# Attention on one core: products for the row maxima issued in pairs behind pairs of score products

## The chip, the cores and the metric

The kernel runs on one core of one Trainium2 chip. The metric is the device time of one execution in microseconds (us). The median of three runs of the kernel before is 5910.59 us (5900.03 to 5910.8).

## The reference

4096 tokens of width 256 go through two layers. What matters here is the attention, which is computed three times: once in the first layer, in a sparse form, and twice in the second layer, in a full causal form.

```
L0:  scores of a query against its own block of 128 keys and every 8th key of all tokens; causal; softmax
L1a: rotary attention:   softmax(causal(Q K^T / 4)) V
L1b: RMS-normed Q and K: softmax(causal(Q K^T / 4)) V
```

Each has 16 heads of width 16. Around them stand layer norms, a quantised product, projections and four experts with a top-2 router; the change doesn't touch them.

## The kernel before, in words

The program runs in stages one after the other: an embedding stage, `attend` for the sparse attention (job 0), a middle stage, `attend` for the two dense attentions together (jobs 1 and 2), and the experts. Only `attend` (L480) is touched, and it is used for both the sparse and the dense stage.

**Units and steps.** A unit is 4 heads (a group) by 512 queries (a strip, number j). The sparse stage has 32 units, the dense stage 64 (8 groups of 8 strips; j runs up in one group and down in the next). A unit is cut into steps of 128 keys: 4(j+1) steps in the dense stage, 1152 in all, and 5 in the sparse one, 160 in all. The last four steps of a dense unit are diagonal: their products are narrower and have a small triangle product added.

**What a step does.** TensorE makes four score products, one for each head, called S0 to S3 below (L712 dense, L719 sparse), with keys as rows and queries as columns. S0 and S1 fill one pair of PSUM banks, S2 and S3 the other (banks 0 to 3). ScalarE takes the exponential of one pair at a time (L770). TensorE then multiplies the exponentials with the values in fp32 (the "weigh" product, called W below, L750, bank 4), one step behind the scores.

**The maxima.** The scores are products of bf16 parts with 96 rows; the softmax needs the maximum of every query row before the exponentials. So every score is made a second time with queries as rows and keys as columns: a "tile" of 128 queries by up to 512 keys, called T below (L686 dense, L676 sparse, L689 and L677 for the masks), and VectorE reduces it to one maximum per row (L799 dense, L789 to L795 sparse). This runs ahead of the scores by `lead(n)` steps, mostly 36 in the dense stage. The tiles go through three PSUM banks in turn (banks 5 to 7): entry e uses bank 5 + e % 3 and waits (L668) until VectorE has finished with entry e - 3. Two other kinds of entry share these three banks, once in each unit: "hand" (L694), which turns the finished negated maxima so that they can be written into the three extra rows of the queries, and "out" (L698), which turns the finished output for the division.

**The order of the work** is written out once as a list, `order` (L506 to L545), which TensorE, VectorE and SyncE all walk. `emit_tiles(goal)` (L510) appends tiles until `goal` of them stand in the list. Inside a step the call at L537 comes behind every score product, with a goal that is one higher each time. So a usual step of TensorE reads S0 T0 S1 T1 S2 T2 S3 T3 W. The first step of a unit has no W behind its products, and the last has two. "out" is appended behind S3 of the second step of a unit (L535), "hand" behind the sixth tile of a unit (L519), and "negate" (L523), VectorE's five small operations that form the negated maximum, behind a unit's last tile.

Of the kernel before, what the change touches and what calls it, by code (L numbers as in the profile page):

```python
# [76 lines left out]
def _build(nc, ctx, d, out):  # L77
# [402 lines left out]
    def attend(jobs, stage, splits, past):  # L480
# [17 lines left out]
        def lead(n):  # L498
            if sparse:
                return sizes[0] + 2  # L500
            if n >= len(units) - STRIPS:
                return sizes[n] + 4
            return min(max(sizes) + 4, 10 + int((2 * BLOCKS * (ends[n] - sizes[n])) ** 0.5))
# [6 lines left out]
        def emit_tiles(goal):  # L510
            nonlocal at
            while at < min(goal, len(ahead)):
                n, tile = ahead[at]
                first_tile = at == 0 or ahead[at - 1][0] != n
                if first_tile:
                    order.append(("queries", n + 1, None))
                order.append(("tile", n, tile))
                of_unit = at - 4 * (ends[n] - sizes[n])
                if of_unit == 5 and n >= 1:  # L519
                    order.append(("hand", n - 1, None))  # L520
                at += 1
                if at == 4 * ends[n]:
                    order.append(("negate", n, None))  # L523
                    if n == len(units) - 1:
                        order.append(("hand", n, None))

        for n in range(len(units)):
            emit_tiles(4 * (ends[n] - sizes[n] + lead(n)))
            emit_tiles(4 * ends[n] + 6)
            order.append(("unit", n, None))  # L530
            for c in range(sizes[n]):
                m = ends[n] - sizes[n] + c
                for h in range(GROUP):
                    order.append(("score", n, (m, c, h)))
                    if n >= 1 and c == 1 and h == 3:  # L535
                        order.append(("out", n - 1, None))
                    emit_tiles(4 * (m + lead(n)) + h + 1)  # L537
                if c >= 1:
                    order.append(("weigh", n, (m - 1, c - 1)))
            order.append(("weigh", n, (m, c)))  # L540
            if n == 0 or n % STRIPS == STRIPS - 1:
                group = 1 if n == 0 else n // STRIPS + 2
                if group < len(groups):
                    order.append(("keys", group, None))
# [8 lines left out]
        with ExitStack() as st:  # L553
# [283 lines left out]
            def attend_pool():  # L837
                tiles, loaded, chunks = splits
                for i, (src, high, low) in enumerate(chunks):
# [15 lines left out]
    middle_early = ExitStack()  # L855
    stage3 = [sbuf(middle_early, f"stage3_{i}", [P, 3 * DIM]) for i in range(2)]
    attend((0,), "sparse", (stage3, [sem(f"stage3_in{i}") for i in range(2)], [
        chunk for name, src, n_out in (("wproj0", d["L0_attn_c_proj_w"], DIM), ("w_rotary", d["L1_attn_Wqkv"], 3 * DIM),
                                       ("w_moe_qkv", d["moe_qkv"], 3 * DIM))
# [495 lines left out]
    for tile, src in ((wo[:], d["L1_ffn_wo"].rearrange("(c p) n -> p c n", p=P)[:, :, MASKED:DIM]),  # L1355
                      (wp[:], d["L1_attn_Wproj"].rearrange("(c p) n -> p c n", p=P)),
                      (n2[:], d["L1_ffn_n2_w"].partition_broadcast(P)), (lower[:], d["c_lower"])):
        sp.dma_start(tile, src).then_inc(final_weights, 16)
    attend((1, 2), "dense", (stage5, [sem(f"stage5_in{i}") for i in range(2)], [
        chunk for name, n_out in (("gate_w", EXPERTS), ("e0_up", HID), ("e2_l1", HID), ("e1_w1", HID), ("e1_w2", HID))  # L1360
        for chunk in matrix(early, name, d["L1_ffn_" + name], DIM, n_out)]), GROUPS * STRIPS)
# [485 lines left out]
```

How the kernel before makes its waits and increments, by code:

```python
    def settle(self):  # L56
        self.engine.wait_ge(self.sem, self.n)
# [56 lines left out]
    def stage_end(finals):  # L114
        for engine in (pe, dve, act, pool, sp):
            for last_sem, value in finals:
                engine.wait_ge(last_sem, value)
# [60 lines left out]
        def embed_sp():  # L178
# [9 lines left out]
                              (scales[:, 0:1], d["L0_ffn_input_scale"].partition_broadcast(P)),  # L188
                              (scales[:, 1:2], d["L0_ffn_kernel_scale"].partition_broadcast(P))):
                sp.dma_start(tile, src).then_inc(weights_in, 16)
            w_view = d["L0_attn_c_attn_w"].rearrange("(c p) n -> p c n", p=P)
            for c in range(DC):
                sp.dma_start(stage[c][:], w_view[:, c, :]).then_inc(stage_in[c], 16)
            for s in range(STRIPS):
                if s + 1 < STRIPS:
                    n = s + 1
                    if n >= 3:
                        sp.wait_ge(base_stored[n % 3], 16 * (n // 3))
                    sp.dma_start(xs[n % 3][:], rows_of(d["L0_attn_hidden_states"], n)).then_inc(x_in[n % 3], 16)
                sp.wait_ge(v_biased, 4 * (s + 1))
                for g in range(GROUPS):
                    dst = v_d[0][g, s * STRIP:(s + 1) * STRIP, :].rearrange("(b p) n -> p b n", p=P)
                    sp.dma_start(dst, ves[s % 2][:, :, g * GROUP * GCOL:(g + 1) * GROUP * GCOL]).then_inc(v_stored[s % 2], 16)
                sp.wait_ge(p3_set, 2 * (s + 1))
                for i, part in enumerate((p1, p2, p3)):
```

## Time and profile before

| | |
|---|---|
| median of three runs | 5910.59 us |
| profiled execution | 5916.0 us |
| its span, first to last instruction | 5914.2 us |
| mean granted TensorE clock | 0.909 of full speed |
| TensorE busy | 5481.3 us, 93% |
| VectorE busy | 4209.3 us, 71% |
| ScalarE busy | 2931.1 us, 50% |

The span's stages, by the groups of instructions and the slices: embedding to about 300 us, sparse attention to about 1370 us, the middle stage to about 1810 us, dense attention to about 5170 us, experts to the end. In the rows below PE is TensorE's matmul, PEld its weight load, DVE VectorE, ACT ScalarE, SP SyncE. A matmul's row lasts from its issue to its modelled end, so rows of neighbouring matmuls overlap; the chain of work gives each only the time by which it moves the end on.

### The profile page before, as it was taken

How to read it: one execution, taken by the hardware profiler on the slowest of the kernel's cores; microseconds unless marked ns; L12 is line 12 of the kernel's file. 1: busy time of each engine (PE TensorE's matmuls, PEld its weight loads, DVE VectorE, ACT ScalarE, POOL GpSimd, SP SyncE). 2: the span in 40 equal slices, each digit the busy share in tenths (PEclk: the TensorE clock that was granted, in tenths of full speed). 3: DMA queues.
4: the chain of work that ended last, by engine and by line, in shares of the span. 5: the costliest groups of instructions: out<-in, count | busy, mean ns of one | idle time of the engine just before them, and what ended most of it. 6: DMA issues, size and time to landing. Idle time of an engine off the chain costs nothing.

```text
span 5914.2 us, 80510 instructions
## 1 busy us (share of the span) xinstructions
PE 5481.3 (93%) x32000; PEld 2459.4 (42%) x32000; DVE 4209.3 (71%) x8394; ACT 2931.1 (50%) x3357; POOL 327.1 (6%) x304
## 2 busy tenths in 40 slices
PE   5499999997665999999999999999999999899999
PEld 4333333334552333333333333333333333378888
DVE  7554444455775888888888888888888887465555
ACT  3223233333332556666666666666666666622332
POOL 2100000001550000000000000000000000020000
PEclk8667677788876999999999999999999999989999
DMA  3631312002546002002002002020120000110110
GB/s 119 143 59 23 50 22 45 19 15 79 161 146 117 15 10 45 12 19 50 9 8 44 11 19 49 8 43 9 19 51 8 8 8 8 30 56 19 36 36 8
DMA packets 268674, 242.18 MB, mean 41 GB/s; under 512 B 73213, under 2 KB 247805, under 8 KB 264061
## 3 DMA queue, kind: packets, MB, share of 16 engines
q1 hardware_dynamic: 268296, 237.02, 17.9%
q8 instruction: 253, 4.15, 0.3%
q14 instruction: 125, 1.02, 0.1%
HBM read 143.49 MB, written 92.27 MB: 40 GB/s over the span
## 4 chain that ended last, share of the span: by engine, by line
PE 84%; DVE 8%; SPq 2%; ACT 2%; issue 2%; DMA 1%; POOL 0%; ACTq 0%; DVEq 0%; POOLq 0%
PE psum L750 21%; PE psum L712 17%; PE psum L686 16%; PE psum L73 12%; PE psum L676 7%; PE psum L719 3%; DVE maxes_dense L799 2%; PE psum L698 1%; SPq L604 1%; PE psum L715 1%; PE psum L689 1%; PE psum L1485 1%; SPq L590 1%; PE psum L724 1%; PE psum L722 1%
## 5 line engine op out<-in xcount | busy, mean ns | idle before, releaser
L799 DVE TENSOR_REDUCE maxes_dense<-psum 128x1 f32<-128x512 f32 (+3 forms) x4608 | 2708.3, 640 | 509.0 <-PE psum L686 296.6
L770 ACT ACTIVATE probs_dense<-psum 128x1024 f32<-128x1024 f32 (+3 forms) x2304 | 2100.5, 951 | 1108.1 <-PE psum L712 820.4
L686 PE MATMUL psum<-keys_dense,queries_dense 96*128 96x512 bf16 (+3 forms) x4608 | 1692.7, 369 | 68.3 <-DMA queries_dense<-parts_scratch 55.8
L712 PE MATMUL psum<-queries_dense,keys_dense 99*128 99x512 bf16 (+3 forms) x4608 | 1668.6, 367 | 8.1 <-ACT probs_dense L770 6.8
L750 PE MATMUL psum<-probs_dense,values_dense 128*32 128x512 f32 (+3 forms) x9216 | 1133.9, 569 | 0.0
L712 PEld LDWEIGHTS psum<-queries_dense,keys_dense 99*128 99x128 bf16 x4608 | 448.0, 98 | 1164.9 <-ACT probs_dense L770 878.4
L686 PEld LDWEIGHTS psum<-keys_dense,queries_dense 96*128 96x128 bf16 x4608 | 452.0, 98 | 532.2 <-DVE maxes_dense L799 260.4
L676 PE MATMUL psum<-keys_sparse,queries_sparse 96*128 96x512 bf16 x512 | 545.4, 1070 | 53.4 <-DMA queries_sparse<-parts_scratch 53.4
L789 DVE TENSOR_REDUCE maxes_sparse<-psum 128x1 f32<-128x144 f32 (+23 forms) x512 | 221.8, 433 | 485.1 <-PE psum L677 485.0
L770 ACT ACTIVATE probs_sparse<-psum 128x1024 f32<-128x1024 f32 x224 | 229.2, 1025 | 483.4 <-PE psum L727 174.0
L1592 ACT ACTIVATE activated<-psum 128x512 f32<-128x512 f32 x208 | 124.5, 599 | 421.5 <-PE psum L73 410.3
L750 PEld LDWEIGHTS psum<-probs_dense,values_dense 128*32 128x32 f32 x9216 | 187.5, 108 | 349.6 <-issue 300.2
L719 PE MATMUL psum<-queries_sparse,keys_sparse 99*128 99x512 bf16 x512 | 241.1, 474 | 23.6 <-DMA queries_sparse<-neg_rows_sparse 22.9
L689 PE MATMUL psum<-tri_query,ident_bf 128*128 128x128 bf16 x1024 | 227.1, 222 | 0.0
L715 PE MATMUL psum<-tri_key,ident_bf 128*128 128x128 bf16 x1024 | 224.6, 221 | 0.0
L719 PEld LDWEIGHTS psum<-queries_sparse,keys_sparse 99*128 99x128 bf16 x512 | 73.9, 146 | 351.2 <-issue 296.9
L791 DVE TENSOR_REDUCE maxes_sparse<-psum 128x1 f32<-128x496 f32 (+9 forms) x496 | 205.6, 415 | 0.0
L1727 DVE CAST hid_high<-activated 128x512 fp32r<-128x512 f32 x208 | 91.5, 440 | 144.8 <-ACT activated L1592 142.0
L750 PE MATMUL psum<-probs_sparse,str_values 128*32 128x512 f32 x1024 | 192.2, 834 | 0.0
L770 ACT ACTIVATE probs_sparse<-psum,after_bias 128x1024 f32<-128x1024 f32 x96 | 106.5, 1115 | 157.3 <-PE psum L719 157.3
L1771 POOL CAST e_down_high<-stage 128x192 fp32r<-128x192 f32 (+1 forms) x10 | 3.6, 358 | 2764.4 <-DMA stage<-in_L_ffn_e_down 2764.4
L1729 DVE TENSOR_TENSOR hid_low<-activated,hid_high 128x512 fp32r<-128x512 f32 x208 | 150.5, 723 | 7.2
(297 smaller groups left out, 5834.9 us busy)
## 6 DMA issues: line engine op xcount, KB each, us to landing
parts_scratch<-part SPq DMA_DIRECT2D x72, 512.0 KB, 4.1
v_scratch<-ve_s SPq DMA_DIRECT2D x96, 256.0 KB, 2.8
queries_dense<-parts_scratch SPq DMA_DIRECT2D x384, 64.0 KB
keys_dense<-parts_scratch SPq DMA_DIRECT2D x42, 512.0 KB, 17.2
keys_sparse<-parts_scratch SPq DMA_DIRECT2D x24, 512.0 KB, 18.9
queries_sparse<-parts_scratch SPq DMA_DIRECT2D x192, 64.0 KB
ao_scratch<-aos_dense SPq DMA_DIRECT2D x64, 128.0 KB, 2.0
ao_s<-ao_scratch SPq DMA_DIRECT2D x16, 512.0 KB, 4.7
```

Of the source, the lines that this page charges most:

```text
L73: m = pe.matmul(out_ap, left(l, c), right(r, c), start=(n == 0), stop=(n == len(pairs) - 1))
L676: pe.matmul(bank, q[0:TROWS, h, b * P:(b + 1) * P], k[0:TROWS, h, STRIDE - 1::STRIDE], start=True, stop=False)
L686: m = pe.matmul(bank[:, 0:width], q[0:TROWS, h, b * P:(b + 1) * P], k[0:TROWS, h, kc * STRIP:kc * STRIP + width], start=True, stop=kc != j)
L689: m = pe.matmul(bank[:, b * P:(b + 1) * P], ident_bf[:], tri_query[:], start=False, stop=True)
L712: m = pe.matmul(full[:, first_col:STRIP], k[:, h, c * P:(c + 1) * P], q[:, h, first_col:STRIP], start=True, stop=not diagonal)
L715: m = pe.matmul(full[:, first_col:first_col + P], ident_bf[:], tri_key[:], start=False, stop=True)
L719: m = pe.matmul(full, k[:, h, c * P * STRIDE + STRIDE - 1:(c + 1) * P * STRIDE:STRIDE], q[:, h, :], start=True, stop=not partly)
L750: m = pe.matmul(psum[own_rows, 4, cols], vt, probs[(2 * m_at + h // 2) % 6][:, h % 2, cols], start=(c == 0), stop=(c == sizes[n] - 1 and b ...
L770: act.activation(probs[i % 6][:, :, first_col:STRIP], psum[:, at2:at2 + 2, first_col:STRIP], ACT.Exp, scale=SCALE, **extra).then_inc(exp_d ...
L789: m = dve.tensor_reduce(mx[:, h * BLOCKS + b, 0:1], bank[:, 0:after], AX.X, ALU.max)
L791: m = dve.tensor_reduce(mx[:, h * BLOCKS + b, 2:3], bank[:, after:NSTR], AX.X, ALU.max)
L799: m = dve.tensor_reduce(mx[:, h * BLOCKS + b, kc:kc + 1], bank[:, 0:width], AX.X, ALU.max)
```

## The change

Inside a step the tiles are appended behind the second and the fourth score product only. The goal there is the same as before, so each call appends two tiles.

```
                     order.append(("score", n, (m, c, h)))
                     if n >= 1 and c == 1 and h == 3:
                         order.append(("out", n - 1, None))
-                    emit_tiles(4 * (m + lead(n)) + h + 1)
+                    if h % 2 == 1:
+                        emit_tiles(4 * (m + lead(n)) + h + 1)
                 if c >= 1:
                     order.append(("weigh", n, (m - 1, c - 1)))
```

A usual step of TensorE reads S0 S1 T0 T1 S2 S3 T2 T3 W. Every instruction is kept, with its operands; the entries keep their order among each other but for "out", which now comes ahead of both tiles T2 and T3 of its step, where it came between them.

## Rows read from the trace of the kernel before

**Rows 1.** The page: busy times, and the granted clock in 40 slices of 148 us.
```profile
PE 5481.3 (93%) x32000; PEld 2459.4 (42%) x32000; DVE 4209.3 (71%) x8394; ACT 2931.1 (50%) x3357; POOL 327.1 (6%) x304
PEclk8667677788876999999999999999999999989999
```

**Rows 2.** Busy time by stretch: stretch, us, busy by engine (instructions), clock, DMA share, GB/s.
```profile
444.00:592.00 148.00, 148.00 (x721) 48.60 (x720) 71.09 (x187) 47.41 (x48) 5.28 (x4) 0.76 0.11 24
...
1036.00:1184.00 148.00, 148.00 (x683) 49.43 (x680) 69.93 (x182) 45.79 (x46) 0.00 (x0) 0.70 0.09 18
...
2072.00:2220.00 148.00, 146.53 (x798) 46.39 (x798) 130.17 (x222) 87.60 (x93) 1.87 (x2) 0.93 0.05 10
...
2960.00:3108.00 148.00, 147.95 (x898) 48.77 (x900) 129.76 (x221) 98.94 (x108) 0.00 (x0) 1.00 0.05 8
```

**Rows 3.** The chain of waits that ended last, one dense step and its neighbours.
```profile
3001.24 0.32 PE psum L712
3001.57 0.22 PE psum L686
...
3002.88 0.22 PE psum L686
3003.10 0.99 PE psum L750 x8
3004.09 0.32 PE psum L712
```

**Rows 4.** The timeline of the same step, in order of time.
```profile
3001.40 0.38 PE L686 MATMUL psum<-keys_dense,queries_dense 96*128 96x512 bf16 x1
3001.82 2.48 DVE L799 TENSOR_REDUCE maxes_dense<-psum 128x1 f32<-128x512 f32 x4 [0.36 <-PE psum L686]
3002.04 1.94 ACT L770 ACTIVATE probs_dense<-psum 128x1024 f32<-128x1024 f32 x2 [0.91 <-PE psum L712]
3002.57 0.10 PEld L686 LDWEIGHTS psum<-keys_dense,queries_dense 96*128 96x128 bf16 x1 [0.19 <-DVE maxes_dense L799]
3002.72 0.38 PE L686 MATMUL psum<-keys_dense,queries_dense 96*128 96x512 bf16 x1
```

**Rows 5.** The timeline of VectorE alone, narrowed to single reductions of that step.
```profile
3001.82 0.69 DVE L799 TENSOR_REDUCE maxes_dense<-psum 128x1 f32<-128x512 f32 x1 [0.36 <-PE psum L686]
3002.43 0.68 DVE L799 TENSOR_REDUCE maxes_dense<-psum 128x1 f32<-128x512 f32 x1
```

**Rows 6.** The timeline in a run of tiles with no scores between them.
```profile
2002.27 0.68 DVE L799 TENSOR_REDUCE maxes_dense<-psum 128x1 f32<-128x512 f32 x1
2003.01 0.10 PEld L686 LDWEIGHTS psum<-keys_dense,queries_dense 96*128 96x128 bf16 x1 [0.50 <-DVE maxes_dense L799]
2003.01 0.39 PE L686 MATMUL psum<-keys_dense,queries_dense 96*128 96x512 bf16 x1 [0.21 <-DVE maxes_dense L799]
```

**Rows 7.** The chain, in the step with "hand".
```profile
2953.30 0.22 PE psum L686
...
2954.44 0.25 PE psum L686
2954.69 0.22 PE psum L712
2954.91 0.38 PE psum L686
2955.29 0.99 PE psum L750 x8
```

**Rows 8.** The timeline behind "negate", and behind "out".
```profile
2950.85 2.48 DVE L799 TENSOR_REDUCE maxes_dense<-psum 128x1 f32<-128x512 f32 x4
...
2951.59 0.10 PEld L686 LDWEIGHTS psum<-keys_dense,queries_dense 96*128 96x128 bf16 x1 [0.39 <-DVE maxes_dense L799]
...
2911.14 1.29 DVE L799 TENSOR_REDUCE maxes_dense<-psum 128x1 f32<-128x512 f32 x2 [0.20 <-PE psum L686]
```

**Rows 9.** The chain in the sparse stage.
```profile
810.86 0.90 PE psum L676
...
812.03 0.22 PE psum L722
...
814.95 0.46 PE psum L719
815.40 0.88 PE psum L676
```

More of the change, by code:

```diff
@@ L536, in attend @@
                         order.append(("out", n - 1, None))
-                    emit_tiles(4 * (m + lead(n)) + h + 1)
+                    if h % 2 == 1:
+                        emit_tiles(4 * (m + lead(n)) + h + 1)
                 if c >= 1:
```

## The prediction

> **What bounds the kernel now.** I read the page first. TensorE is busy for 93% of the span, VectorE for 71%, ScalarE for 50% [rows 1]. The busy time by stretch then says that this differs by stage: in the dense stage, here 2960 to 3108 us, TensorE is busy for 147.95 of 148 us at full clock and VectorE for 129.76; in the sparse stage VectorE is busy for half and TensorE for all, at a clock of 0.70 to 0.76 [rows 2]. A busy TensorE row can hide waits, so the third view is the chain of waits inside one dense step. It never leaves TensorE: S0 moves the end on by 0.32 us, each of the seven products behind it by 0.22 (3001.57 to 3003.10 is 1.53 us for seven, 0.219 each), W by 0.99 [rows 3]. A step takes 0.32 + 1.53 + 0.99 = 2.85 us. ScalarE idles 0.91 us in it and VectorE 0.36 [rows 4].
>
> The fourth view, the timeline of that step, shows how close VectorE is. T0 ends at 3001.40 + 0.38 = 3001.78 and its reduction starts at 3001.82, 0.04 later. T3 goes into T0's bank (three banks, L666 to L668), and its weight load came at 3002.57, with "VectorE" as what ended its idle time [rows 4]. The reduction of T0 had ended at 3001.82 + 0.69 = 3002.51 [rows 5]. So the wait was real, but it cost nothing: a product that starts from a late weight load ends 0.39 us behind it [rows 6], which would be 3002.96, and the chain has T3's end at 3003.10 anyway. The bank loop has 0.14 us to spare.
>
> **The change, part by part.**
>
> *Nothing is added or removed.* The same products, reductions and exponentials run, with the same operands. SyncE's list moves by at most one score product (which it doesn't issue), so its transfers stay where they are: nothing for them.
>
> *The pairs of scores finish one slot earlier.* S1 ends 0.22 us sooner behind S0, so each first exponential may start 0.22 us sooner. In a usual step ScalarE idles 0.91 us and no product waits for it in the chain [rows 3, 4]. Worth nothing.
>
> *Three tiles on, the bank comes back too late.* This is the term that decides. From the end of T0 to the end of T3 the bank loop needs 0.04 (to the reduction) + 0.69 (it) + 0.06 (its end to the weight load) + 0.39 (load to end of T3) = 1.18 us [rows 4 to 6]. Before, six products end in that time (S1 T1 S2 T2 S3 T3): 6 x 0.219 = 1.31, so nothing is lost. After, five do (T1 S2 S3 T2 T3): 5 x 0.219 = 1.09. T3 comes 0.08 to 0.09 us late, and W and the next S0 stand behind it on TensorE. The loop closes in every step: from T3's end over W 0.99, S0 0.32, S1 0.22, T0 0.22 to T0's end, and 1.18 to the next T3: 2.93 us against 2.85. VectorE's four reductions need 2.48 [rows 4], so it isn't the bound.
>
> How often, by following L527 to L545: of the 1152 dense steps 634 have full score products, four full tiles, and neither "hand" nor "out". About 45 of them follow a "negate": there the reductions begin when VectorE has done its small operations (2950.85) and T3's load already waits for that (2951.59) [rows 8], in both orders alike. The other 589 pay 0.082: **48 us**.
>
> *Steps with "hand"* with full tiles (54). "hand" takes a bank, so T3 needs T1's reduction, the second of the row: from the end of T0 (2953.52) to the end of T3 (2955.29) it is 1.77 us by the chain, bank-bound already [rows 7]. Here the added S1 ahead of T0 comes through whole: 54 x 0.22 = **12 us**.
>
> *Steps with "out"* (49 with full tiles). The step itself is bound by VectorE, with no wait to add. But VectorE then idles 0.20 us until the next step's T0 is there [rows 8]; T0 comes one slot later. In that next step 0.22 takes the place of the 0.08 counted above: 49 x 0.14 = **7 us**.
>
> *Diagonal score steps* with full tiles. I shorten the products to 0.055 us per 128 columns (0.22 a full one) and add 0.055 for the triangle. First of the four (35): the added triangles give TensorE 3.07 us a step, the loop needs 3.04: nothing. Second (31): as a full step, 0.08. Third (36): TensorE 2.63, loop 2.65 before and 2.82 after: 0.165. Fourth (35): 2.41 by four reductions at 0.60 before, 2.47 after: 0.06. Together 2.5 + 6 + 2 = **10 us**.
>
> *Diagonal tiles* (some 250 steps). T0 is then 128 wide, its reduction short, and T3 has its bank in time: nothing. Steps with no tiles (the last ones) and bursts of tiles (the first units) read the same in both orders: nothing.
>
> *The sparse stage.* A tile product takes 0.90 us in the chain and a score 0.22 to 0.46 [rows 9], so from T0 to T3 there are about three tiles and two scores, over 3 us, and the bank is long free. The wait costs nothing. But the granted clock there lies at 0.70 to 0.76, between its two levels of 1.2 and 2.4 GHz, and the tile product takes 0.90 at one and 0.88 at the other (the score of 0.46 stands beside the 0.88) [rows 9]. Two such products side by side could shift the share of the levels either way. The stretch at 0.76 gets through 721 matmuls and that at 0.70 through 683 [rows 2], 5.5% for six hundredths; over some 890 us with tiles that is about 8 us for a hundredth. I take no shift, and keep two hundredths, 16 us, each way for the range.
>
> **Sum**: 48 + 12 + 7 + 10 = 77 us. Against the profiled execution, 5916.0, that is 5993; that execution is 5.4 us above the median of the runs, 5910.59, so I forecast 5988.
>
> *The ends.* The 0.082 is a small difference of sums, each term read to a hundredth. Its lower end is a loop of 1.13 (stall 0.04), 589 x 0.04 = 24 in place of 48, so about 5963. The upper end is a whole slot: the usual step of before has its load at 3002.57 and its start at 3002.72, 0.15 apart [rows 4]. If T3 needed that lead too, it would end 0.53 behind its load, 1.32 after T0, and the stall be 0.22: 130 in place of 48, about 6070. The run of tiles shows the load and the product both at 2003.01 when TensorE has really been waiting [rows 6], so I take 0.39.
>
> The Trainium skill (TensorE: Matmul & The Clock Gate, Back-to-back issue gap) gives about 131 ns as the sustained spacing of load and matmul pairs of 512 columns. By it five slots would be 0.66 us and the stall half a microsecond a step. The trace has 0.219 us [rows 3], and the sum goes by that.
>
> **The rivals.**
>
> *Hidden (0.07).* The loop is really short enough: the ends of matmuls are modelled, and an error of 0.08 in 1.18 us would leave no stall. What is left is the part with "hand" and "out", 19 us at most if those hold, near nothing if they don't. 5911 to 5920. Against it: load and reduction are measured rows, and the row of T3's load already shows VectorE as releaser.
>
> *A whole slot (0.12).* As above, 6070; or part of it.
>
> *The dense clock drops (0.05).* TensorE now stops for 0.08 us in each step. If the grant fell as in the stretch 2072 to 2220, 0.93 [rows 2], where bursts of tiles make TensorE wait, some 2900 us of TensorE-bound steps would take 7% longer, 200 us more: about 6190. Against it: the steps with "hand" wait longer than 0.08 and lie in stretches at 1.00 [rows 2, 7]. The Trainium skill (TensorE: Matmul & The Clock Gate, A second HAM failure mode) says that short idles between groups of matmuls while cycling through PSUM banks can make the clock swing. This rival is that rule; the stretches at 1.00 speak against it so far.
>
> *Faster, by the sparse clock (0.06).* Place: the sparse stage, where tile products that gain nothing from the clock now stand in twos and scores in twos. Price: 8 us a hundredth. It decides once the stage's mean rises by about 0.10, from 0.73 to 0.83, which pays back the 77 us; at 0.86 the time is 5988 - 104 = 5884. For it: the grant does move there. Against it: each step holds the same products as before, in nearly the same places.
>
> **How the numbers follow.** The forecast has 0.70. The range takes in its lower end, the sparse clock's 16 us, and about half the way to the whole slot: 5947 to 6045. Outside lie the dense clock, the far part of the whole slot, the hidden case and the faster one. A measurement can tell 0.2%, about 12 us, from no change. Faster by more than that: 0.06; within it: 0.07; slower: 0.87.
>
> **What would show it.** In a usual dense step of the new kernel the chain shows T3 at about 0.30 us instead of 0.22, with the reduction of the tile three before it as what ended the load's wait, and steps of 2.93 us; VectorE's idle time in a step grows from 0.36 to about 0.44. The reductions wait longer in total by some 70 us, and the dense stage is longer by as much, the others by nothing. The forecast is wrong if T3 stays at 0.22 (hidden), shows 0.44 (whole slot), if the dense clock is below 1.00, or if the sparse stage moves by over 16 us.

## The result, and the profile after

The changed kernel is slower: 5975.69 us (median of four runs, 5967.47 to 5980.03) against 5905.37 us for the kernel before (four runs, 5900.03 to 5910.8). The ratio is 1.0117, 95% interval 1.010 to 1.0135. The forecast was 5988 in 5947 to 6045, with 77 us more; it is 70.

The page of the changed kernel (line numbers are one higher from L538 on: the tiles' product is L687, the scores' L713, W L751, the reduction L800), to be read beside [rows 1]:

```profile
PE 5506.2 (92%) x32000; PEld 2444.9 (41%) x32000; DVE 4178.7 (70%) x8394; ACT 2920.9 (49%) x3357; POOL 327.8 (5%) x304
PEclk8677777788877999999999999999999999999999
PE 80%; DVE 12%; SPq 2%; issue 2%; ACT 2%; DMA 1%; POOL 0%; ACTq 0%; DVEq 0%; POOLq 0%
```

The engines' work is what it was and the clock didn't fall (mean granted clock 0.917, before 0.909). What is new is in the last row, the share of each engine in the chain that ended last: VectorE has 12% of it, where the page of before has

```profile
PE 84%; DVE 8%; SPq 2%; ACT 2%; issue 2%; DMA 1%; POOL 0%; ACTq 0%; DVEq 0%; POOLq 0%
```

Next the chain in a usual dense step, beside [rows 3] (like neighbours stand in one row here):

```profile
3000.91 0.54 PE psum L713 x2
3001.45 0.43 PE psum L687 x2
3001.88 0.43 PE psum L713 x2
3002.32 0.53 PE psum L687 x2
3002.84 0.99 PE psum L751 x8
3003.84 0.54 PE psum L713 x2
```

S0 and S1 take 0.54, T0 and T1 0.43, S2 and S3 0.43, but T2 and T3 0.53: T3 alone is 0.10 over the others. The step lasts 3003.84 - 3000.91 = 2.93 us, as forecast, against 2.85. The timeline of that step, beside [rows 4], says what T3 waited for:

```profile
3001.70 2.48 DVE L800 TENSOR_REDUCE maxes_dense<-psum 128x1 f32<-128x512 f32 x4 [0.44 <-PE psum L687]
...
3002.45 0.10 PEld L687 LDWEIGHTS psum<-keys_dense,queries_dense 96*128 96x128 bf16 x1 [0.41 <-DVE maxes_dense L800]
```

T0's reduction starts at 3001.70 and takes 0.69 us, to 3002.39; T3's weight load follows at 3002.45; T3 ends at 3002.84. VectorE isn't short of time: it idles 0.44 us in each step instead of 0.36. Both engines wait longer, for each other. Over the dense stage and what borders on it, from 1790 to 5260 us, the waits of tiles' weight loads for VectorE (us in total, times, longest) add up to

```profile
PEld psum L687 <- DVE maxes_dense L800: 460.9, 1127, 0.8
```

where before it was

```profile
PEld psum L686 <- DVE maxes_dense L799: 260.4, 1010, 0.8
```

Not each of these microseconds moves the end on, as [rows 4] showed. The reductions' own waits for TensorE grew too, over the same stretch. Before and after they read, for tiles without a mask:

```profile
DVE maxes_dense L799 <- PE psum L686: 296.6, 709, 22.1
DVE maxes_dense L800 <- PE psum L687: 367.8, 737, 20.8
```

That is 71 us more, near the 70 that the forecast gave as a sign. Behind the masks of diagonal tiles they grew by 45 us besides (188.6 to 234.1), so all in all by more than it said.

**Where the 64 us between the two profiled executions are** (5978.2 against 5914.2 us of span): I take a stage from the start of its first tile product to the start of its last output copy. These are the rows of the two lines in the view of a line, first the dense ones of the kernel before, then those of the changed kernel; the two times in each are the first and last start.

```profile
L775 ACT ACTIVATE outs_dense<-psum x64: 597/598/600, 1866.8 to 5150.9; 128x512 f32<-128x512 f32 x64
L686 PE MATMUL psum<-keys_dense,queries_dense x4608: 219/379/634, 1808.4 to 5114.3; 96*128 96x512 bf16 x168, 96*128 96x128 bf16 x24
...
L776 ACT ACTIVATE outs_sparse<-psum x32: 597/597/599, 348.5 to 1390.8; 128x512 f32<-128x512 f32 x32
L677 PE MATMUL psum<-keys_sparse,queries_sparse x512: 1056/1061/1087, 286.7 to 1358.1; 96*128 96x512 bf16 x171
L776 ACT ACTIVATE outs_dense<-psum x64: 597/597/599, 1858.4 to 5218.2; 128x512 f32<-128x512 f32 x64
L687 PE MATMUL psum<-keys_dense,queries_dense x4608: 218/380/635, 1802.8 to 5181.6; 96*128 96x512 bf16 x168, 96*128 96x128 bf16 x24
```

| stage | before | after |
|---|---|---|
| sparse | 283.5 to 1395.2: 1111.7 | 286.7 to 1390.8: 1104.1 |
| dense | 1808.4 to 5150.9: 3342.5 | 1802.8 to 5218.2: 3415.4 |

The dense stage is 72.9 us longer. The sparse one is 7.6 us shorter, and no other part of the span moved by more than 3.3 us. How long a sparse stage lasts without any change to it is a matter of the runs below.

### The profile page after: what moved, and what is told of

Same layout as the page of the kernel before. It is cut to its first block, busy times and chain, and to the rows that moved or that the text cites. A ratio compares the mean times of both kernels' runs of the same rounds, so it can differ in the third digit from the quotient of the medians.

```text
span 5978.2 us, 80510 instructions
## 1 busy us (share of the span) xinstructions
PE 5506.2 (92%) x32000; PEld 2444.9 (41%) x32000; DVE 4178.7 (70%) x8394; ACT 2920.9 (49%) x3357; POOL 327.8 (5%) x304
## 4 chain that ended last, share of the span: by engine, by line
PE 80%; DVE 12%; SPq 2%; issue 2%; ACT 2%; DMA 1%; POOL 0%; ACTq 0%; DVEq 0%; POOLq 0%
PE psum L751 20%; PE psum L713 16%; PE psum L687 15%; PE psum L73 11%; PE psum L677 7%; DVE maxes_dense L800 6%; PE psum L720 3%; SPq L605 1%; PE psum L690 1%; PE psum L716 1%; PE psum L1486 1%; SPq L591 1%; PE psum L725 1%; PE psum L699 1%; PE psum L680 1%
## 5 line engine op out<-in xcount | busy, mean ns | idle before, releaser
L800 DVE TENSOR_REDUCE maxes_dense<-psum 128x1 f32<-128x512 f32 (+3 forms) x4608 | 2679.9, 639 | 605.3 <-PE psum L687 367.8
L687 PE MATMUL psum<-keys_dense,queries_dense 96*128 96x512 bf16 (+3 forms) x4608 | 1455.7, 370 | 97.3 <-DMA queries_dense<-parts_scratch 53.5
L713 PE MATMUL psum<-queries_dense,keys_dense 99*128 99x512 bf16 (+3 forms) x4608 | 1341.0, 366 | 7.2 <-ACT probs_dense L771 6.8
L751 PE MATMUL psum<-probs_dense,values_dense 128*32 128x512 f32 (+3 forms) x9216 | 1133.4, 569 | 0.0
L713 PEld LDWEIGHTS psum<-queries_dense,keys_dense 99*128 99x128 bf16 x4608 | 368.9, 97 | 1096.7 <-ACT probs_dense L771 802.1
L687 PEld LDWEIGHTS psum<-keys_dense,queries_dense 96*128 96x128 bf16 x4608 | 443.2, 98 | 836.4 <-DVE maxes_dense L800 460.9
L677 PE MATMUL psum<-keys_sparse,queries_sparse 96*128 96x512 bf16 x512 | 509.2, 1063 | 54.1 <-DMA queries_sparse<-parts_scratch 54.1
L751 PEld LDWEIGHTS psum<-probs_dense,values_dense 128*32 128x32 f32 x9216 | 188.0, 108 | 271.7 <-ACT probs_dense L771 201.8
L720 PE MATMUL psum<-queries_sparse,keys_sparse 99*128 99x512 bf16 x512 | 210.4, 478 | 23.4 <-DMA queries_sparse<-neg_rows_sparse 22.7
L690 PE MATMUL psum<-tri_query,ident_bf 128*128 128x128 bf16 x1024 | 214.9, 222 | 0.0
L716 PE MATMUL psum<-tri_key,ident_bf 128*128 128x128 bf16 x1024 | 206.3, 221 | 0.0
L751 PE MATMUL psum<-probs_sparse,str_values 128*32 128x512 f32 x1024 | 189.2, 821 | 0.0
L677 PEld LDWEIGHTS psum<-keys_sparse,queries_sparse 96*128 96x128 bf16 x512 | 58.5, 114 | 277.4 <-issue 189.9
L796 DVE TENSOR_REDUCE maxes_sparse<-psum 128x4 f32<-128x512 f32 x128 | 84.7, 690 | 111.2 <-PE psum L683 110.8
```

Of the source, the lines that this page charges most:

```text
L677: pe.matmul(bank, q[0:TROWS, h, b * P:(b + 1) * P], k[0:TROWS, h, STRIDE - 1::STRIDE], start=True, stop=False)
L687: m = pe.matmul(bank[:, 0:width], q[0:TROWS, h, b * P:(b + 1) * P], k[0:TROWS, h, kc * STRIP:kc * STRIP + width], start=True, stop=kc != j)
L690: m = pe.matmul(bank[:, b * P:(b + 1) * P], ident_bf[:], tri_query[:], start=False, stop=True)
L713: m = pe.matmul(full[:, first_col:STRIP], k[:, h, c * P:(c + 1) * P], q[:, h, first_col:STRIP], start=True, stop=not diagonal)
L716: m = pe.matmul(full[:, first_col:first_col + P], ident_bf[:], tri_key[:], start=False, stop=True)
L720: m = pe.matmul(full, k[:, h, c * P * STRIDE + STRIDE - 1:(c + 1) * P * STRIDE:STRIDE], q[:, h, :], start=True, stop=not partly)
```

## The experiments

Each ran beside the kernel before on the same chip, in three groups; the first group (dense pairs, short reductions, one pair) ran on another chip than the rest. In the diffs only the lines in which a kernel differs from the kernel before are shown. Stages are measured as above.

**Pairs in one stage only.** Dense alone:

```
-                    emit_tiles(4 * (m + lead(n)) + h + 1)
+                    if h % 2 == 1 or sparse:
+                        emit_tiles(4 * (m + lead(n)) + h + 1)
```

> Pairs in the dense stage only; the sparse stage keeps one tile behind each score. Bank loop (theory): all of the loss sits in the dense stage, so the whole kernel is slower than before by 70 to 80 us, ratio 1.012 to 1.014, the chain in a usual dense step shows 2.93 us, and the sparse stage is as long as before (about 1112 us from its first tile to its last output copy). Rival, that the sparse stage matters too: the changed kernel's sparse stage was 8 us shorter at a clock of 0.77 instead of 0.75; if the pairs did that, this kernel is about 8 us slower than the changed one.

Measured: 5983.95 us against 5904.78, ratio 1.0134 (1.0121 to 1.0147). The dense stage is 3416.4 us long (1811.9 to 5228.3), that of the changed kernel 3415.4; the sparse stage 1113.8 us.

Sparse alone:

```
-                    emit_tiles(4 * (m + lead(n)) + h + 1)
+                    if h % 2 == 1 or not sparse:
+                        emit_tiles(4 * (m + lead(n)) + h + 1)
```

> Pairs in the sparse stage only. Bank loop (theory): nothing waits for a bank there, so the time is that of before within the swing of the sparse stage, which was 1090 to 1115 us long in kernels that all had the same sparse code: ratio 0.997 to 1.003. Rival, that pairs lift the sparse clock: 8 us or more under before, ratio 0.9985 or less, with the granted clock of 300 to 1370 us above 0.75.

Measured: 5897.03 us against 5905.01 (medians), ratio 0.9996 (0.9984 to 1.0008). The ratio isn't that of the medians, which would be 0.9986. Sparse stage 1099.9 us (285.5 to 1385.4), dense 3341.4. The whole loss sits in the dense stage. The sparse stage with pairs, 1104.1 and 1099.9, lies inside what it does without them in the other kernels here, 1090.5 to 1125.6. Its length goes with the granted clock of 300 to 1370 us. These are the stretches of two kernels with the same sparse code, the one with inner pairs and the one with W ahead of the last tile, both below (columns as in [rows 2]):

```profile
300.00:1370.00 1070.00, 1044.27 (x5052) 338.12 (x5053) 520.86 (x1395) 352.00 (x349) 12.87 (x12) 0.77 0.19 33
```
```profile
300.00:1370.00 1070.00, 1045.23 (x4861) 339.66 (x4863) 510.21 (x1366) 333.62 (x330) 12.85 (x12) 0.73 0.19 32
```

0.77 goes with 1090.5 us and 0.73 with 1125.6. That is 35 us for four hundredths, 9 us a hundredth where the forecast had 8. So a comparison of two single profiles can't tell a change of less than some 35 us in the whole time, and from here on I compare dense stages.

Whether the pairs gain a little in the sparse stage stays open. For it: both kernels with sparse pairs have a granted clock of 0.77 there, the one with sparse pairs alone has a median 8 us under the kernel before, and dense pairs alone came out 8 us over the changed kernel, as the rival of the first run had said. Against it: the kernel with one inner pair, below, has 0.77 without sparse pairs, and the intervals of the ratios overlap (1.0100 to 1.0135 and 1.0121 to 1.0147; 0.9984 to 1.0008 takes in no change). A gain of more than some 9 us lies outside the interval.

**The same pairs with a shorter reduction.** If the bank loop is the cause, the loss must vanish when VectorE gives the bank back 0.13 us sooner. With pairs:

```
-                    emit_tiles(4 * (m + lead(n)) + h + 1)
+                    if h % 2 == 1 or sparse:
+                        emit_tiles(4 * (m + lead(n)) + h + 1)
...
-                           ACT.Exp, scale=SCALE, **extra).then_inc(exp_done, 1)
+                           ACT.Exp, scale=SCALE if sparse else SCALE / 8, **extra).then_inc(exp_done, 1)
...
-                            m = dve.tensor_reduce(mx[:, h * BLOCKS + b, kc:kc + 1], bank[:, 0:width], AX.X, ALU.max)
+                            seen = min(width, 384) if kc < j else width
+                            m = dve.tensor_reduce(mx[:, h * BLOCKS + b, kc:kc + 1], bank[:, 0:seen], AX.X, ALU.max)
```

> Pairs in the dense stage, and the reductions of full off-diagonal tiles read 384 of the 512 columns (the maxima then leave out the last 128 columns of such tiles, and the dense exponentials have an eighth of their scale, so that they stay finite). A reduction should fall from 0.69 to about 0.56 us, the loop from 1.18 to 1.05 us, under the 1.09 of five products. Bank loop: T3 goes back to 0.22 in the chain, a usual step takes 2.85 us, and the time is within 30 us of the single order with the same short reductions. Rival, that the pairing itself costs (two products of a kind side by side, or the exponentials): the step stays at 2.93 and the distance to that kernel stays at 70 us.

Both kernels leave out the last 128 of a full tile's 512 columns, and with them part of what the maximum is for: their times are there to be compared with each other, not to be used. The control has the last two edits and the order of before.

> The order of before with the same short reductions (384 of 512 columns, and an eighth of the scale in the dense exponentials): the control. Bank loop: the usual step was bound by TensorE with 0.14 us to spare, so it stays at 2.85 us; only the steps with hand, out and those bound by VectorE get shorter, in all 10 to 30 us less than before. Rival, that VectorE's total work sets the pace: 3500 reductions less 0.13 us each would take off over 100 us.

Measured: 5851.36 us with pairs (ratio 0.9910, 0.9897 to 0.9923), 5857.05 in the single order (0.9918, 0.9906 to 0.9931). The dense stages are 3289.1 and 3288.2 us: 73 us apart with full reductions, 1 us with short ones. This 1 us is a balance: the 561 usual steps with pairs are 6 us shorter in all and those with "out" 4 us, while the 26 plain steps with "hand" still take 3.26 us against 3.12, and those behind "negate" and the last diagonal ones are longer too. The chain of the pairs, in a usual step:

```profile
3019.89 0.54 PE psum L713 x2
3020.43 0.43 PE psum L687 x2
3020.86 0.43 PE psum L713 x2
3021.30 0.43 PE psum L687 x2
3021.73 0.99 PE psum L751 x8
3022.72 0.54 PE psum L713 x2
```

T2 and T3 take 0.43 again and the step 2.83 us. The timeline of this kernel has the load of T3 still waiting for VectorE, but without effect, just as before the change:

```profile
3020.68 1.95 DVE L801 TENSOR_REDUCE maxes_dense<-psum 128x1 f32<-128x384 f32 x4 [0.61 <-PE psum L687]
3021.29 0.10 PEld L687 LDWEIGHTS psum<-keys_dense,queries_dense 96*128 96x128 bf16 x1 [0.28 <-DVE maxes_dense L801]
```

The control answers the other question too. 3500 reductions less 0.13 us each are over 450 us of VectorE's work; they take off 54 us of the dense stage (3342.5 to 3288.2). VectorE's total isn't the bound of either order. It was more than the 10 to 30 us that I expected: the steps with "hand", "out" and diagonal scores depend on it more than I had counted.

**One pair, six products apart.** Dense steps read S0 T0 S1 S2 T1 T2 S3 T3 W.

```
-                    emit_tiles(4 * (m + lead(n)) + h + 1)
+                    if sparse or h != 1:
+                        emit_tiles(4 * (m + lead(n)) + h + 1)
```

> Dense steps read S0 T0 S1 S2 T1 T2 S3 T3 W: one pair of tiles and one of scores, but T0 and T3 are six products apart as before, and no tile is behind S1. Bank loop: no loss in a usual step, 2.85 us; the whole within 12 us of before. Rival, that the side-by-side products cost by themselves: about half of the loss, 35 us, ratio 1.006. The second pair of scores starts two slots earlier than in the single order; if the exponentials held it up, S2 would show a wait for ScalarE.

Measured: 5902.78 us, ratio 0.9996 (0.9985 to 1.0007); dense stage 3342.5 us, to the tenth that of before. That it agrees so well is chance: the usual steps are 4 us shorter in all, and the steps with "hand", "out" and behind "negate" take it back. The chain:

```profile
3003.49 0.99 PE psum L751 x8
3004.49 0.32 PE psum L713
3004.81 0.22 PE psum L687
3005.03 0.43 PE psum L713 x2
3005.46 0.43 PE psum L687 x2
3005.89 0.22 PE psum L713
3006.11 0.22 PE psum L687
3006.33 0.99 PE psum L751 x8
```

Tiles in a pair cost nothing in a usual step here. What matters is how many products lie between a tile and the third one behind it.

**A larger dose.** All four tiles stand behind the fourth score.

```
-                    emit_tiles(4 * (m + lead(n)) + h + 1)
+                    if h == 3 or sparse:
+                        emit_tiles(4 * (m + lead(n)) + h + 1)
```

> A larger dose: in the dense stage all four tiles stand behind the fourth score, S0 S1 S2 S3 T0 T1 T2 T3 W. Bank loop: T3's end over W 0.99, S0 0.32, S1 to S3 0.65, T0 0.22 to T0's end, and 1.18 to T3's end: 3.36 us for a usual step, against 2.85 before and 2.93 with pairs. With 561 such steps 290 us more, and with what the other steps with full tiles lose 350 to 450 us in all, ratio 1.06 to 1.08. Rival, that the loss goes with the number of changes between scores and tiles: this order has fewer than the pairs, and would be at or under 2.93 us.

Measured: 6368.92 us, ratio 1.0792 (1.0768 to 1.0816). The dense stage is 3807.3 us long (1796.5 to 5603.8), 465 us more, a little over the 350 to 450 expected. The chain from one W to the next in a usual step:

```profile
3241.53 0.99 PE psum L751 x8
3242.53 0.97 PE psum L713 x4
3243.50 0.23 PE psum L687
3243.73 0.02 issue
3243.75 0.70 DVE maxes_dense L800
3244.45 0.04 issue
3244.50 0.39 PE psum L687
3244.89 1.00 PE psum L751 x8
```

3244.89 - 3241.53 = 3.36 us, as worked out ahead. Here the whole loop stands in the chain: T0's end at 3243.73, 0.02 to the reduction, 0.70 for it, 0.05 to the load, 0.39 to T3's end, 1.16 in all. The terms that the forecast took from rows of before, 1.18 in all, hold within 0.02 us each.

**W in another place.** I expected a better kernel from this. Pairs, with W in the middle:

```
-                    emit_tiles(4 * (m + lead(n)) + h + 1)
-                if c >= 1:
+                    if h % 2 == 1 or sparse:
+                        emit_tiles(4 * (m + lead(n)) + h + 1)
+                    if c >= 1 and h == 1 and not sparse:
+                        order.append(("weigh", n, (m - 1, c - 1)))
+                if c >= 1 and sparse:
```

> Pairs in the dense stage with W moved to the middle of the step: S0 S1 T0 T1 W S2 S3 T2 T3. Bank loop: W now stands between T0 and T3, but from T2 to the next step's T1 there are only five products (T3 S0 S1 T0 T1) and no W, so the wait moves from T3 to T1 and stays 0.08 us: a usual step takes 2.93 us again, 45 us lost over the usual steps; the steps with hand, whose bank-bound stretch now has W in it, give back some 10 to 20 us, so ratio 1.005 to 1.010. Rival, that what costs is T2 and T3 right ahead of W (or any wait that ends at W): the loss is gone, 2.85 us.

Pairs, with W ahead of the last tile:

```
-                    emit_tiles(4 * (m + lead(n)) + h + 1)
-                if c >= 1:
+                    if sparse or h == 1:
+                        emit_tiles(4 * (m + lead(n)) + h + 1)
+                    elif h == 3:
+                        emit_tiles(4 * (m + lead(n)) + 3)
+                        if c >= 1:
+                            order.append(("weigh", n, (m - 1, c - 1)))
+                        emit_tiles(4 * (m + lead(n)) + 4)
+                if c >= 1 and sparse:
```

> Pairs in the dense stage with W ahead of the last tile: S0 S1 T0 T1 S2 S3 T2 W T3. Bank loop: W stands in three of the four stretches between a tile and the third one behind it, and the fourth (T3 to the next T2) has seven products, 1.53 us against 1.18. No wait is left in a usual step: 2.835 us as with the short reductions, 90 us under the changed kernel; steps with hand fall from 3.3 us to about 3.0. In all 15 to 40 us under before, ratio 0.993 to 0.998. Rival, that pairs cost by themselves: above 1.005.

The single order, with W ahead of the last tile:

```
-                    emit_tiles(4 * (m + lead(n)) + h + 1)
-                if c >= 1:
+                    if sparse or h < 3:
+                        emit_tiles(4 * (m + lead(n)) + h + 1)
+                    else:
+                        if c >= 1:
+                            order.append(("weigh", n, (m - 1, c - 1)))
+                        emit_tiles(4 * (m + lead(n)) + 4)
+                if c >= 1 and sparse:
```

> The single order in the dense stage with W ahead of the last tile: S0 T0 S1 T1 S2 T2 S3 W T3. Bank loop: from T3 to the next T2 there are six products, 1.31 us against 1.18, the other stretches have W in them. A usual step stays at 2.846 us; steps with hand and out get shorter as in the pairs with W ahead, so 10 to 35 us under before, and 5 to 10 us above those pairs. Rival, that the gain of that kernel came from the pairs and not from the place of W: this one is at before.

Measured, in this order: ratios 1.0239 (1.0217 to 1.0261), 1.0025 (1.0008 to 1.0042) and 1.0090 (1.0070 to 1.0111). The forecasts for the usual step held, as the chain of each shows: 2.93 us with W in the middle, 2.835 with pairs and W ahead, 2.85 in the single order. The totals missed: dense stages of 3479.4, 3359.7 and 3392.8 us. In the two kernels with W ahead of the last tile, much of what I had left out stands at the end of each unit's tiles. With W in the middle 137 us are lost, of which usual steps explain some 45; I haven't taken the rest apart. This is the timeline of the pairs with W (L756) ahead of the last tile, around "negate":

```profile
2970.56 0.69 DVE L805 TENSOR_REDUCE maxes_dense<-psum 128x1 f32<-128x512 f32 x1 [0.82 <-PE psum L695]
...
2971.29 0.27 DVE L816 TENSOR_REDUCE neg_dense<-maxes_dense 128x16 f32<-128x112 f32 x1
...
2972.31 0.68 DVE L805 TENSOR_REDUCE maxes_dense<-psum 128x1 f32<-128x512 f32 x1
```

The last tile of the unit is behind W, so VectorE idles 0.82 us while W runs, and its reduction and the small operations come only then: three tiles of the next unit stand in the banks by the time it is free, at 2972.31. In the kernel before, the same operations (2949.83 to 2950.85) began while W was running, from 2948.99 to 2950.06. The wait had been covered by W and is now in the open: from one end of W to the next, the 26 plain steps with "hand" take 3.76 us instead of 3.31. The last steps of units get longer too (35 with full tiles, 2.74 us instead of 2.40). That W's place matters by what VectorE has in hand when W begins is my reading of these rows; no run isolates it.

**"hand" and "out" moved out of the loop.** In the order of before:

```
+                of_unit = at - 4 * (ends[n] - sizes[n])
+                if of_unit == 8 and n >= 1 and not sparse:
+                    order.append(("hand", n - 1, None))
                 order.append(("tile", n, tile))
-                of_unit = at - 4 * (ends[n] - sizes[n])
-                if of_unit == 5 and n >= 1:
+                if of_unit == 5 and n >= 1 and sparse:
...
-            emit_tiles(4 * ends[n] + 6)
+            emit_tiles(4 * ends[n] + (6 if sparse else 9))
...
-                    if n >= 1 and c == 1 and h == 3:
+                    if n >= 1 and (c, h) == ((1, 3) if sparse else (2, 0)):
```

> The order of before, with two dense entries moved: hand from behind the sixth tile of a unit to ahead of its ninth (behind W, at the start of a step), and out from the second step's end to the third step's start, behind S0. Bank loop: both no longer stand between a T0 and its T3, so the step with hand falls from 3.31 us to about 3.05, and the dense stage is 10 to 25 us shorter than 3343 us. Rival, that VectorE's backlog at a unit's start sets these steps wherever the entries are: no change.

The same moves, with the line of the inner pair (`if sparse or h != 1:` ahead of the last `emit_tiles`):

> The same two moves with S0 T0 S1 S2 T1 T2 S3 T3 W, whose usual step takes 2.840 us instead of 2.846. Bank loop and the shorter slot of like products: 3 to 5 us under the single order with the moves, the best of all.

Measured: ratios 1.0006 (0.9996 to 1.0015) and 1.0003 (0.9990 to 1.0016), dense stages 3343.7 and 3346.1 us: no gain. The chain shows one half of it working (L696 is "hand"):

```profile
2947.93 0.99 PE psum L752 x8
2948.93 0.32 PE psum L714
2949.25 0.17 PE psum L696
2949.42 0.32 PE psum L688
...
2951.05 0.99 PE psum L752 x8
```

The step with "hand" is 2951.05 - 2947.93 = 3.12 us instead of 3.31. The first two steps of the 31 plain units with "out" fall too, from 7.48 to 6.92 us together, but the steps into which "hand" and "out" moved rise by as much: the 46 plain third steps of units go from 2.85 to 3.65 us. That VectorE's work for "out" only moved, and is wanted near a unit's start wherever it stands, is how I read it; it stays open. None of the orders tried beats the kernel before by more than can be measured.

## Why the prediction was right, step by step

The trace tells the term of each kind of step: the time from the end of one W to the end of the next, averaged over all dense steps of a kind (the first step of a unit has no W and is counted with the second). Times are in us. The kinds that aren't listed are longer by about 6 us in all, and the time from the first tile to the first W is 3 us shorter; with these the last column adds up to the 73 us of the stage.

| kind of step (full tiles) | steps | before | after | forecast a step | measured in all |
|---|---|---|---|---|---|
| usual | 561 | 2.846 | 2.927 | +0.082 | +45.1 |
| with "hand" | 26 | 3.309 | 3.525 | +0.22 | +5.6 |
| first two, with "out" | 31 | 7.475 | 7.665 | +0.08 | +5.9 |
| behind "negate" | 26 | 2.889 | 3.072 | 0 | +4.7 |
| first diagonal scores | 25 | 3.078 | 3.072 | 0 | -0.1 |
| second | 25 | 2.866 | 2.939 | +0.08 | +1.8 |
| third | 35 | 2.450 | 2.620 | +0.165 | +5.9 |
| fourth | 35 | 2.400 | 2.517 | +0.06 | +4.1 |
| first two, with both, behind "negate" | 15 | 6.612 | 6.459 | +0.22 | -2.3 |
| diagonal tiles, full scores | 151 | 2.759 | 2.753 | 0 | -0.8 |

- **The bank loop** is shown: it is in the chain; the loss in a usual step vanishes with a shorter reduction and with six products from T0 to T3, and the step grows to 3.36 us with three. Its price was 0.081 a step against 0.082. (The stall itself is 0.09, against the 2.835 us of pairs with short reductions; products in pairs give back 0.01 of it.) The Trainium skill's 131 ns spacing (TensorE: Matmul & The Clock Gate, Back-to-back issue gap) isn't what this trace has after the change either: 0.43 us for two.
- **The whole slot** (0.22 us of stall) is refuted: T3 ended 0.39 behind its load.
- **"hand"** was right where it stands alone, 0.216 against 0.22, but 15 of the 54 steps that I counted are second steps of a unit that also have "out"; these got shorter by 0.15 us a pair of steps. The term of 12 us measured about 8 for the 39 steps outside them.
- **"negate" was priced wrongly.** "In both orders alike" failed: these steps lost 0.18 us. A unit's last four tiles are narrow to wide; in the pair order T0 and T1 come later, so the wide tile's reduction queues behind its neighbours, and the small operations start later. The delay shows in the traces: where a "negate" comes in a step with full scores (36 of them), its first operation starts 0.23 us ahead of the end of W before and 0.05 ahead of it after, and the next reduction is later by the same 0.19. That the queue of narrow tiles is what delays it is my reading of the order. Six further such steps with diagonal scores bring it to about 6 us.
- **"out"** was priced in the wrong place. I had put 0.22 in place of 0.08 on the step behind it, since VectorE idles there [rows 8]; the 46 plain third steps of units lost 0.081, like any other. The loss came in the first two steps, 0.19 us a pair where I had 0.08: 31 x 0.11 = 3 us more than forecast there, in place of 7 behind it.
- **Diagonal scores**: three of four kinds within 0.01 us; the fourth cost 0.12 and not 0.06. In all 12 us against 10.
- **The pairs of scores** gained nothing: ScalarE isn't in the chain of a usual step before or after, as said.
- **The dense clock** stayed at 1.00 in the stretch of [rows 2], 2960 to 3108 us, and was at 1.00 also with four tiles in a row, where TensorE stops for half a microsecond in each step. The first of these is the changed kernel, the second the one with four tiles:

```profile
2960.00:3108.00 148.00, 146.51 (x878) 47.78 (x882) 124.44 (x219) 95.42 (x104) 0.00 (x0) 1.00 0.05 8
```
```profile
3256.00:3404.00 148.00, 134.21 (x777) 41.66 (x777) 108.35 (x195) 85.21 (x91) 0.00 (x0) 1.00 0.25 40
```

  The rule that micro-idles make the clock swing (the Trainium skill, same page, A second HAM failure mode) had no part in these stretches.
- **The sparse stage** moved by 7.6 us between the two profiles, inside the 16 that I had allowed, and not by the pairs.

So the dense sum came to 73 us instead of 77 by errors that partly cancel: "hand" and "out" too high, "negate" and the fourth diagonal step too low. The usual step carries 45 of it, and that is the part that was understood; that the rest came within 4 us of its sum is partly luck. Of the 12 us by which 5988 lies over the median, 5 come from the median of the kernel before, 5905.37 here where the forecast started from 5910.59. One slip stands beside the sum: with 19 us for "hand" and "out" the hidden case would reach 5930, not 5920. The forecast doesn't rest on it.

## What to carry to other kernels

Where n buffers go round between two engines, count the work that the producer has between use e and use e + n, in the order as issued, and compare it with the consumer's loop: end of the product, reduction, load, end of the next. Neither engine's busy share shows it, and a wait row with some slack behind it is the warning. Whoever moves a long instruction must also look at what the other engine did under its cover, at the rare steps too: three reorderings had the usual step that was forecast for them and lost in the others.

## What the runs showed that I had not expected

- Two neighbouring products of a kind take 0.43 us in the chain, 0.2165 each, where scores and tiles in turn take 0.219. With the stall out of the way this gives 2.835 us a step instead of 2.846 (the pairs with short reductions, 561 steps). Scores have 99 rows and tiles 96; whether that is the reason wasn't tried.
- The sparse stage of one and the same code lasted between 1090.5 and 1125.6 us, at mean granted clocks of 0.77 and 0.73.
